# One regrouping of the carried state, a split signal and a reordered drain in a fused embedding, attention, state-space and expert kernel

## The reference

```python
x = emb[tokens] * sqrt(256) + pos_enc
qk = einsum('bqd,bkd->bqk', x @ w_q, x @ w_k) / sqrt(256)
h = einsum('bqk,bkd->bqd', softmax(qk, axis=1), x @ w_v)

u = layernorm(h)                       # and the mixer on it:
zxbcdt = (layernorm(u) * ln_w + ln_b) @ in_proj_w.T
dt = softplus(zxbcdt[..., -8:] + dt_bias)
xs, B, C = split(silu(conv4(xBC)))     # 512 channels of x, 128 of B, 128 of C
# two chunks of 128 tokens in a row of 256, 8 heads of 64:
#   Y_diag = (C B^T * exp(segsum(dt*A))) (dt*xs)      inside a chunk
#   states = B^T (decay * dt*xs)                      what chunk 0 leaves
#   Y_off  = exp(cumsum(dt*A)) * (C states)           what chunk 1 gets of it
Y = Y_diag + Y_off + D * xs
y = Y * silu(z);  y = y * rsqrt(mean(y*y) + 1e-5) * norm_w
h = h + (y @ out_proj_w.T + u)

scores = softmax(layernorm(h) @ w_router); top 2 of 8
slot = expert * 1024 + (how many earlier choices of this expert)   # kept if < 1024
h = h + sum over the two: weight * gelu(xb @ w1[e]) @ w2[e] + bias
```

## Time and profile before

| | |
|---|---|
| median of 3 runs | 925.45 us (925.26 to 925.67) |
| the profiled execution | 926.9 us, its span 925.2 us |
| granted TensorE clock, mean | 0.996 |
| part one, to the end of the last scatter's issue | to 539.8 us |
| part two, first real product to the end | 548.5 to 925.2 us |
| busy PE, PEld, DVE, ACT, POOL | 98, 87, 68, 57, 54% |

### The profile page before, as it was taken

How to read it: one execution, slowest core, us unless ns; L and a number is a source line. 1 busy time by engine, 2 the same in 40 slices (tenths; PEclk the granted TensorE clock), 3 DMA queues, 4 the chain that set the end, 5 groups by cost and what they waited for, 6 DMA issues and landing times. The chain is left out here.

```text
span 925.2 us, 17776 instructions
## 1 busy us (share of the span) xinstructions
PE 904.3 (98%) x5832; PEld 806.5 (87%) x5832; DVE 633.4 (68%) x1698; ACT 528.6 (57%) x1097; POOL 503.8 (54%) x498
## 2 busy tenths in 40 slices
PE   8999999999999999999999979999999999999998
PEld 7888798888888888888888779999999999999997
DVE  1587889888988898889889644646464646464633
ACT  1767776677667766776667434444443434343533
POOL 5656877887778777876775522223232323232343
PEclk9999999999999999999999989999999999999999
DMA  7940011001000000000000044343434342523221
GB/s 211 321 154 17 30 47 34 23 34 34 13 23 14 24 13 23 14 25 12 12 14 5 25 138 122 70 109 74 108 70 112 67 115 63 119 58 79 23 58 46
DMA packets 49398, 59.13 MB, mean 64 GB/s; under 512 B 6304, under 2 KB 44683, under 8 KB 49360
## 3 DMA queue, kind: packets, MB, share of 16 engines
q1 hardware_dynamic: 35920, 42.14, 14.1%
q0 software_dynamic: 13440, 16.50, 10.7%
HBM read 33.62 MB, written 30.67 MB: 69 GB/s over the span
## 5 line engine op out<-in xcount | busy, mean ns | idle before, releaser
L690 POOL DMA_INDIRECT out<-ye,tok_slot x56 | 96.0, 1713 | 250.0 <-DMA out<-ye,tok_slot 128.0
L973 ACT ACTIVATE hf<-bank 128x512 f32<-128x512 f32 x128 | 79.3, 620 | 187.1 <-PE bank L1814 187.0
L1423 DVE TENSOR_TENSOR h_lo<-hf,h_hi 128x512 fp32r<-128x512 f32 x128 | 88.8, 694 | 101.5 <-ACT h_hi L975 100.1
L1812 PE MATMUL bank<-w_hi,h_hi 128*128 128x256 f32 x512 | 146.1, 285 | 0.0
L1813 PE MATMUL bank<-w_lo,h_hi 128*128 128x256 f32 x512 | 144.9, 283 | 0.0
L1814 PE MATMUL bank<-w_hi,h_lo 128*128 128x256 f32 x512 | 144.9, 283 | 0.0
L1122 DVE SCALAR_TENSOR_TENSOR xc<-bank,cw,xc 128x253 f32<-128x253 f32 (+2 forms) x288 | 128.2, 469 | 1.9 <-ACT xc L799 0.4
L1812 PE MATMUL bank<-xe_hi,w_hi 128*128 128x512 f32 x256 | 100.0, 391 | 0.0
L1813 PE MATMUL bank<-xe_lo,w_hi 128*128 128x512 f32 x256 | 99.8, 390 | 0.0
L1814 PE MATMUL bank<-xe_hi,w_lo 128*128 128x512 f32 x256 | 99.7, 389 | 0.0
L1813 PEld LDWEIGHTS bank<-w_lo,h_hi 128*128 128x128 f32 x512 | 98.3, 192 | 0.0
(11 more groups left out here) (223 smaller groups left out, 2352.3 us busy)
## 6 DMA issues: line engine op xcount, KB each, us to landing
w_raw<-w SPq DMA_DIRECT2D x16, 1024.0 KB
slots_dram<-zero_row SPq DMA_DIRECT2D x1, 8320.0 KB, 29.9
xe<-slots_dram SPq DMA_DIRECT2D x15, 520.0 KB, 4.5
out<-hb SPq DMA_DIRECT2D x16, 256.0 KB, 2.1
w_raw<-in_wT SPq DMA_DIRECT2D x2, 644.0 KB, 6.2
out<-zero_row SPq DMA_DIRECT2D x1, 1024.0 KB, 32.1
slots_dram<-rows,slot POOLq DMA_INDIRECT x64
out<-ye,tok_slot POOLq DMA_INDIRECT x64
```

Of the source, the lines that this page charges most:

```text
L690: g.indirect_dma_start(out, bass.IndirectOffsetOnAxis(ap=tok_slot[q][:, j:j + 1], axis=0), ye[q][:, j, :], None, compute_op=ALU.add).then_ ...
L973: sc.activation(hf[m % 2][:, :], h_bank[i % H_BANKS][:, :], ACT.Gelu_apprx_tanh)\
L1423: vc.tensor_tensor(h_lo[:, m, :], hf[m % 2][:, :], h_hi[:, m, :].bitcast(F32), ALU.subtract)\
L1812: te.matmul(out_, hi, rhi, start=first_, stop=False)
```

## The change

- **Other bracketing.** (C state) with state = B^T xdec becomes (C B^T) xdec. `state_inputs` now multiplies B of chunk 0 with C of chunk 1 in place of the transpose (128x128 both), ScalarE copies it to `across`, and `across_chunks` is one product of 128x512 in place of two; `from_state`, `state`, `st` go. VectorE reads it before the first chunk's y, since `to_yT` writes the same bank, and `to_yT` 0 stands behind the dt product on TensorE.
- **Signals.** `hn_coef` is raised behind `shift`; `normed` waits for it, and `residuals` for `hu_coef` behind `hu_s`.
- **Skips in full halves.** GpSimd's `skip_x` waits for VectorE's second decay product (`m_ready[1]`).
- **Skips in the drain.** GpSimd makes four diagonal matrices of D once (`skip_diag`, in the first full half). TensorE multiplies them with x into the banks of the own products, which accumulate on them; GpSimd's skips and VectorE's two additions of them go there.
- **Drain, otherwise.** VectorE makes the residual and norm of the tail's batch first; the decayed x is made by ScalarE in eight pieces; the own product of chunk 0 stands before the one across; the router of the tail's batch is read ahead of the last batch's norm; the counts of choices stand first in the last half; the last row descriptions are made by VectorE; GpSimd's root of the square mean stands ahead of the segment inputs in the last half with a front. Dummies in the drain are 2 and not 15, in the last half 22 and not 21, ahead of the experts 3 and not 6.

```diff
-        DRAIN = dict(rows=2, seg0=1, seg2=8, state=2, out=2)
-        LAST = dict(v2T=10, route=2, choices=9)
+        DRAIN = dict(rows=2)
+        LAST = dict(first=9, v2T=2, route=2, choices=9)
...
-                g.tensor_tensor(shift[p][:, :, :], lnr[p][:, :, :], bc(lnm[p][:, :].unsqueeze(1), [P, 2, KD]), ALU.mult)
+                g.tensor_tensor(shift[p][:, :, :], lnr[p][:, :, :], bc(lnm[p][:, :].unsqueeze(1), [P, 2, KD]), ALU.mult)\
+                    .then_inc(hn_coef[p], 1)
                 g.tensor_scalar(hu_s[p][:, :], lnr[p][:, 0, :], 1.0, 1.0, ALU.mult, ALU.add).then_inc(hu_coef[p], 1)
...
+            def skip_matrices():
+                g.tensor_tensor(skip_diag[:, :, :].rearrange("p m (j d) -> p m j d", j=2),
+                                bc(ident[:, :].rearrange("p (j d) -> p j d", j=2).unsqueeze(1), [P, KI, 2, HD]),
+                                bc(dskip[:, :].rearrange("p (m j) -> p m j", j=2).unsqueeze(3), [P, KI, 2, HD]),
+                                ALU.mult).then_inc(s_diag, 1)
...
                 if b:
+                    pool.wait_ge(m_ready[KD - 1][q], m_ready[KD - 1].now(b, q))
                     skip_x(b, q, 0)
                     skip_x(b, q, 1)
+                if b and not t:
+                    skip_matrices()
...
-                act.wait_ge(hu_coef[p], hu_coef.now(r, p))
+                act.wait_ge(hn_coef[p], hn_coef.now(r, p))
...
+            def decayed_x(r, p):
+                act.wait_ge(edec_ready[p], edec_ready.now(r, p))
+                act.wait_ge(xdt_ready[p], xdt_ready.now(r, p, 1))
+                for h in range(NH):
+                    at = slice(h * HD, (h + 1) * HD)
+                    ins = sc.activation(xdec[p][:, at], xdt[p][:, 0, at], ACT.Copy, scale=edec[p][:, h:h + 1])
+                ins.then_inc(xdec_ready[p], 1)
...
+                def last_y(r, p):
+
+                    dve.wait_ge(yd_psum[p], yd_psum.now(r, p, 1))
+                    dve.wait_ge(sz_ready[p], sz_ready.now(r, p))
+                    vc.tensor_tensor(y[p][:, 0, :], bank[p][YD_BANK[0]][:, :], sz[p][:, 0, :], ALU.mult)\
+                        .then_inc(y_ready[p], 1)
+                    carried_y(r, p, bank[1 - p][1])
+                    back.wait(carried_y.last)
+                    dve.wait_ge(yd_psum[p], yd_psum.now(r, p))
+                    own = back.mark(vc.tensor_tensor(y[p][:, 1, :], bank[1 - p][3][:, :], y[p][:, 1, :], ALU.add))
+                    gated(r, p, 1, own)
...
-                    te.transpose(bank[where][3][:, 0:P], xc[p][:, KI, 0:P], ident[:, :])
+                    te.matmul(bank[where][3][:, 0:P], xc[p][:, KI, 0:P], xc[p][:, KI + 1, P:2 * P], start=True, stop=True)
...
-                def chunk_state(r, p):
+                def across_chunks(r, p, dst):
...
-                    te.matmul(bank[p][3][:, :], bs[p][:, :], xdec[p][:, :], start=True, stop=True)\
-                        .then_inc(state_psum[p], 1)
+                    te.matmul(dst[:, :], across[p][:, :], xdec[p][:, :], start=True, stop=True)\
+                        .then_inc(yo_psum[p], 1)
...
-                def from_state(r, p):
-                    pe.wait_ge(st_ready[p], st_ready.now(r, p))
-                    pe.wait_ge(decay_ready[p], decay_ready.now(r, p))
-                    te.matmul(bank[p][2][:, :], xc[p][:, KI + 1, P:2 * P], st[p][:, :], start=True, stop=True)\
-                        .then_inc(yo_psum[p], 1)
...
+                def skips(r, p, c):
...
+                    for m in range(KI):
+                        te.matmul((bank[p][YD_BANK[0]], bank[1 - p][3])[c][:, m * P:(m + 1) * P], xc[p][:, m, c * P:(c + 1) * P],
+                                  skip_diag[:, m, :], start=(m == 0), stop=False)
...
-                    keep_clock(0, 6)
+                    keep_clock(0, 3)
```

More of the change, by code:

```diff
@@ L771, in residuals @@
             def residuals(r, p):
+                act.wait_ge(hu_coef[p], hu_coef.now(r, p))
                 for c in range(KD):
@@ L843, in x_rows @@
                 copy(xs[p][:, c, :], bank[p][XS_BANK[c]][:, :], xs_ready[p])
-            def state(r, p):
-                act.wait_ge(state_psum[p], state_psum.now(r, p))
-                copy(st[p][:, :], bank[p][3][:, :], st_ready[p])
             def square(r, p, c):
@@ L889, in half @@
                     decay(b, q, 3)
-                    late_rows(b, q)
-                    state(b, q)
+                    norm_2(t, p)
                     square(b, q, 0)
@@ L933, in half @@
                     normed(f, p)
-                if b:
-                    state(b, q)
                 if f:
@@ L1303, in half @@
                     count_choices(p)
-                    back.close()
                     routing.close()
@@ L1339, in half @@
                     dt_in(f, p)
+                if not f:
+                    describe_rows(t, p)
                 if t:
@@ L1645, in own_chunk, with own_on_skips @@
                     ins.then_inc(yd_psum[p], 1)
-                def from_state(r, p):
-                    pe.wait_ge(st_ready[p], st_ready.now(r, p))
-                    pe.wait_ge(decay_ready[p], decay_ready.now(r, p))
-                    te.matmul(bank[p][2][:, :], xc[p][:, KI + 1, P:2 * P], st[p][:, :], start=True, stop=True)\
-                        .then_inc(yo_psum[p], 1)
+                def skips(r, p, c):
+                    if c == 0:
+                        pe.wait_ge(decay_ready[p], decay_ready.now(r, p, 1))
+                    else:
+                        pe.wait_ge(s_diag, 1)
+                        pe.wait_ge(bs_ready[p], bs_ready.now(r, p))
+                        pe.wait_ge(gm_ready[p], gm_ready.now(r, p))
+                    for m in range(KI):
+                        te.matmul((bank[p][YD_BANK[0]], bank[1 - p][3])[c][:, m * P:(m + 1) * P], xc[p][:, m, c * P:(c + 1) * P],
+                                  skip_diag[:, m, :], start=(m == 0), stop=False)
+                def own_on_skips(r, p, c):
+                    pe.wait_ge(m_ready[c][p], m_ready[c].now(r, p))
+                    pe.wait_ge(xdt_ready[p], xdt_ready.now(r, p, c + 1))
+                    for h in range(NH):
+                        ins = te.matmul((bank[p][YD_BANK[0]], bank[1 - p][3])[c][:, h * HD:(h + 1) * HD], seg[p][:, c, h, :],
+                                        xdt[p][:, c, h * HD:(h + 1) * HD], start=False, stop=(h == NH - 1))
+                    ins.then_inc(yd_psum[p], 1)
                 def to_yT(r, p, c):
@@ L1656, in to_yT, with project_rows @@
                         .then_inc(yT_psum[p], 1)
-                def project_rows(r, p, c, where):
+                def project_rows(r, p, c, where, ks=range(KI)):
                     pe.wait_ge(w_out_ready, 1)
                     pe.wait_ge(yT_ready[p], yT_ready.now(r, p, c + 1))
-                    for k in range(KI):
+                    for k in ks:
                         ins = te.matmul(bank[where][0][:, c * DM:(c + 1) * DM], yT[p][:, c, k, :], w_out[:, k, :],
                                         start=(k == 0), stop=(k == KI - 1))
-                    if c == KD - 1:
+                    if c == KD - 1 and ks[-1] == KI - 1:
                         ins.then_inc(out_psum[p], 1)
@@ L1705, in half @@
                     x_to_rows(b, q, 0)
+                    segment_sums(b, q, 0)
                     x_to_rows(b, q, 1, p)
-                    keep_clock(p, DRAIN["seg0"])
-                    segment_sums(b, q, 0)
                     segment_sums(b, q, 1)
-                    keep_clock(p, DRAIN["seg2"])
+                    skips(b, q, 1)
+                    skips(b, q, 0)
                     segment_sums(b, q, 2)
                     segment_sums(b, q, 3)
-                    keep_clock(p, DRAIN["state"])
-                    chunk_state(b, q)
-                    own_chunk(b, q, 0)
-                    from_state(b, q)
-                    own_chunk(b, q, 1)
+                    own_on_skips(b, q, 0)
+                    across_chunks(b, q, bank[p][1])
+                    own_on_skips(b, q, 1)
                     to_yT(b, q, 0)
+                    to_v2T(t, p)
                     pe.wait_ge(h2_ready[p], h2_ready.now(t, p))
-                    project_rows(b, q, 0, p)
+                    project_rows(b, q, 0, p, range(KI // 2))
                     to_yT(b, q, 1)
-                    keep_clock(p, DRAIN["out"])
+                    project_rows(b, q, 0, p, range(KI // 2, KI))
                     project_rows(b, q, 1, p)
-                    to_v2T(t, p)
                     route(t, p)
@@ L1785, in half @@
                     project_dt(f, p)
+                if b:
+                    to_yT(b, q, 0)
+                if f:
                     project_channels(f, p, 0)
```

81 lines of the change are left out of this document (38 added, 43 removed).

## The result

The changed kernel is slower: 928.99 us (median of seven runs, 926.11 to 930.19) against 925.45 of the kernel before, ratio 1.0031, 95% interval 1.0020 to 1.0042. Forecast were 917.9 and a range of 912.5 to 922.5. The seven runs don't agree as those of before do, and their times follow the mean granted clock of TensorE roughly: 0.989 in the one of 926.11, 0.983 in the two of 930.2, with one of 929.22 at 0.987 out of order. Before has 0.996.

A forecast was written before the change was run, and what follows sets the result against it. VectorE was taken to bound fast halves, TensorE behind late hn the slow ones. Gains 0.2 (start) + 4.0 (loop) + 3.0 (drain) + 0.4 (dummies) = 7.6 us gave 917.9 from 925.45; range 912.5 to 922.5.

The forecast's parts named there:

- What is late next: Loop halves: TensorE will wait some tenths, harmlessly; v comes by VectorE, giving 30.8 us a half, 4.0 off in all.
- The order of carried part and first chunk on VectorE: Loop, VectorE: order turned round with the same operations, priced at nothing.
- the 0.05 for GpSimd's wait: Loop: skips start after VectorE's second decay product; the course to `split_hT` taken as 0.05 us later than the fast half.
- The normed rows' signal: Loop: hn waits for `shift` only; TensorE's wait of 0.64 us goes from the eight slow halves.
- 30.8 forecast for everything: Loop: 22.04 + 0.05 to nmax, 3.28 to the product with the probabilities, 5.44 to the next half.
- The bracketing: Loop: one 128x512 product goes, 0.86 us, its replacement 0.11 dearer; 0.75 us a half off TensorE.
- VectorE's bound: Loop: VectorE, with GpSimd's grip on it, bounds the fast half; TensorE behind the late hn bounds the slow one.
- a rival of 0.05: Drain: fewer dummies and a pause over 1 us drop the clock to 1.2 GHz; 928 us; chance 0.05.
- The drain: From the loop's last own-chunk product to the last scatter: 3.0 us sooner, bounds 1 and 5.
- Dummies ahead of the experts: Ahead of the first expert product: six of 12 dummies go; 0.4 us gained, over 1 if the clock stays full.

The follow-up runs named there:

- 9: Changed kernel without GpSimd's wait for the last decayed scores ahead of the skips, no fill matmuls: 923.31 us, ratio to before 0.9972.
- 11: Changed kernel with the product across the chunks issued where `from_state` stood, old order on VectorE and TensorE, no GpSimd wait: 920.84 us (0.9946).
- experiment 4: Kernel before with the one signal alone: normed rows wait for `hn_coef` behind the shift: 923.68 us (0.9971).
- 6: Kernel of experiment 4 with the `from_state` product cut from 512 to 128 columns, nothing else moved: 923.21 us (0.9969).
- 10: Kernel of experiment 4 with VectorE's carried part ahead of the first y: 929.22 us (1.0052).
- 8: Changed kernel with four unread fill matmuls per full half, and y's transposes back ahead of the dt product: 934.67 us (1.0094).
- 12: Kernel of experiment 4 with the changed kernel's GpSimd wait ahead of the skips added: 924.20 us (0.9983).
- 7: Changed kernel with four unread fill matmuls per full half, without GpSimd's wait ahead of the skips: 920.92 us (0.9953).
- 2: Changed kernel with six dummy matmuls ahead of the first expert products in place of three: 927.39 us (1.0023).
- 3: Changed kernel with 52 matmuls in place of 38 behind the last choices: 927.13 us (1.0010).
- 1: Changed kernel with four unread 128-column matmuls (the fill) where the chunk-state product stood in each full half: 924.45 us (0.9980).
- 14: Kernel of 7 with 52 matmuls in place of 38 behind the last choices: 921.29 us (0.9953).
- experiment 5: Loop of the kernel before with the one signal, plus the drain of the changed kernel: 919.94 us (0.9943).

## Why the prediction was wrong

The step that failed is *What is late next*, in two sentences. "... some tenths each; that costs nothing as long as it is back at the product with the probabilities before v" took TensorE's idle spots as free. "The order of carried part and first chunk on VectorE is turned round with the same operations ...: nothing for both" took a swap for nothing because its sum of work is nothing. A term of the step before it, the 0.05 for GpSimd's wait, was too small as well. In the place of these three terms the runs show 8.2 us: without the wait the changed kernel is at 923.3 (9), and with the old order on VectorE and TensorE as well at 920.8 (11).

- **The normed rows' signal.** Right, and nearly the whole of the loop's true gain: hn's transposes at 1.73, no alternation. Alone it makes the halves 30.85 (experiment 4), against 30.8 forecast for everything, so that sum itself was 0.05 a half too low.
- **The bracketing.** Its gain was put at nothing beyond VectorE's bound, and it is nothing (11; also 6). What it brought along was priced wrongly. The swap delays y's transposes from 4.9 to 5.4 (10; 5.6 in the changed kernel) and costs 5.5 alone, falls included; from 9 to 11 it is 2.5, again with the falls. The dt product ahead of y's transposes hides most of TensorE's lateness (without it: 8), so that the undisturbed halves of 9 are 30.88 for 30.84 in 11, and what the swap costs there is falls. What is left in the changed kernel is a stretch behind the own-chunk products with thin matmuls and two short waits, and the clock falls at its end or among the first channels behind it.
- **The wait ahead of the skips.** Put at 0.05 a half; 0.08 alone (12), 0.10 in the changed kernel (9), 0.19 with the fill (435.5 less 432.9 over 14, in 7), where six halves have ScalarE's late copy. Taking it out of the changed kernel gives 5.7, out of the filled one 3.5, and putting it into the fourth costs 0.5 to 1. In the changed kernel most of its price comes on top of the 0.10 a half, as falls, and the prices of wait and swap don't simply add up.
- **The clock.** I had it as a rival of 0.05, in the drain, and looked for a pause of over 1 us. It came in the loop, at pauses of 0.15 to 0.3. The drain has one as well, but early (495.49), where it makes the stretch to the next own-chunk product 25.3 long for 24.8 in 2 and 3. The fill removes the loop's falls and takes 4.5 us off the median; of the 3.7 between the profiled executions 3.2 are in the loop (1). That the falls are a main cause is shown. What exactly the throttle responds to is not. Missing work without a late y brought none in the trace of 6; a late y with all the work did (10), and with the fill too if TensorE stands in front of it (8); with fill and dt ahead of y together it stayed whole in the loop (1, 7, 14); a hole of 0.61 in another place brought one (11). The Trainium skill (TensorE: Matmul & The Clock Gate, "A second HAM failure mode: psum-queue depth-cycling") tells of short idle times between groups of matmuls that make the clock go up and down. The trace agrees in kind: the fall shown above comes behind a stretch in which TensorE is busy for 2.97 of 3.30 us. The page gives no number for them, and 6 shows that idle time alone doesn't decide.
- **The drain.** Right: 3.0 forecast, 3.2 measured (2.5 in 2 and 3), 2.9 by itself. Its inner steps were off and made up for each other, so the closeness is partly luck: relative to the loop's last own-chunk product y's last operation, which ends at 519.90, is 1.3 sooner and not 1.8, h is 1.4 sooner and not 1.9, and the routing behind it gives the rest.
- **Dummies ahead of the experts.** Forecast 0.4 gained, 1.2 lost behind the last scatter. I had TensorE either in the old fall or out of it. That the fall could come later and cover the products was not among the cases. By 2 halving the dummies isn't its cause, and in 4, with all six, the fall covers the first 1.8 us of the products too (545.19, to 546.97).

Without the mis-priced steps: the kernel of experiment 11, with everything else of the change, is at 920.8, and that of experiment 5, with the signal and the drain alone, at 919.9, within 2 us of the forecast's 917.9. The changed kernel is 9 above the latter.

## What to carry to other kernels

Price a swap by when each result is ready and who stands waiting for it, not by its sum of work; two lines of VectorE cost 5.5 us here. Take a change apart before adopting it: one signal and the drain held all of the gain, and the part with the largest saving on paper held none. When work leaves a nearly full TensorE, read the granted clock per stretch in the new profile, and compare the spread of the runs; a kernel whose runs differ by 0.4% and whose times follow the mean clock is losing it in places.

## What was not expected of the hardware

- The granted clock falls to 1.2 GHz in a loop without a long pause: the stretch of 3.30 us ahead of one fall has TensorE busy for 2.97. It stayed there for 3.41 us each time in the loop, and 3.41 or 6.83 ahead of the experts. A fall in the loop cost 0.9 to 1.3 us in the changed kernel, 1.7 in experiment 10 and 2.0 in experiment 2 (halves of 33.01 and 32.98 beside 31.0).
- The number of falls is not fixed by the program. Seven runs of the changed kernel have mean clocks of 0.983 to 0.989, and the time follows them roughly, by 0.7 us for 0.001 (930.19 less 926.11, over 0.006).
- An operation of GpSimd that is held by VectorE's use of SBUF starts sooner after it than one that waits for its signal: 1.23 to 1.25 against 1.28 to 1.31 after the own-chunk product in most halves (4 and 12). The Trainium skill (SBUF — State Buffer, "Who interferes with whom") has the lock; the 0.05 is this case's.
